# A state-space loop in which GpSimd, no longer VectorE, makes the product of delta and u, from ScalarE's copy of u

## The reference

```python
def fp_step(y_prev):
    x_tilde = (x - y_prev) @ W_mix.T + y_prev                   # "u", 256 channels
    bc = _shift1(y_prev) @ W_bc.T
    Bt = bc_normalize(B0 + bc[..., :16]); Ct = bc_normalize(C0 + bc[..., 16:])
    # h_t = exp(delta_t A) h_{t-1} + (delta_t u_t) B_t ;  y_t = sum_n h_t C_t + D u_t
    y = _selective_scan(x_tilde, delta, A, Bt, Ct, D)
    return layer_norm(y)
y_star = fori_loop(0, 8, lambda i, y: y + 0.99 * (fp_step(y) - y), zeros)
y = fp_step(y_star)
```

## Time and profile before

| | us |
|---|---|
| runs | 10309.9, 10301.13, 10301.96 |
| median | 10301.96 |
| profiled execution, time | 10288.07 |
| profiled execution, span | 10285.8 |

### The profile page before, as it was taken

How to read it: one execution, slowest core, us unless ns; L and a number is a source line. 1 busy time by engine, 2 the same in 40 slices (tenths; PEclk the granted TensorE clock), 3 DMA queues, 4 the chain that set the end, 5 groups by cost and what they waited for, 6 DMA issues and landing times.

```text
span 10285.8 us, 259086 instructions
## 1 busy us (share of the span) xinstructions
PE 9253.0 (90%) x88474; PEld 6391.3 (62%) x88474; DVE 8862.1 (86%) x16781; ACT 7235.6 (70%) x15052; POOL 6118.4 (59%) x4900
## 2 busy tenths in 40 slices
PE   7989899898998989989899899999989999899988
PEld 4656656566565665656656566565665656656566
DVE  6988979789797897978979799797997979879798
ACT  5867768677686776857768576685866858668586
POOL 1936829377293772927729277392763928639286
PEclk9999999999999999999999999999999999999999
DMA  0000000000000000000000000000000000000000
GB/s 22 0 3 1 2 3 0 3 1 2 3 0 3 1 2 3 0 3 1 2 3 0 3 1 2 3 0 3 1 2 3 0 3 1 2 3 0 3 1 3
DMA packets 648478, 23.66 MB, mean 2 GB/s; under 512 B 629185, under 2 KB 647250, under 8 KB 647506
## 3 DMA queue, kind: packets, MB, share of 16 engines
q1 hardware_dynamic: 647890, 16.11, 3.7%
HBM read 9.40 MB, written 4.19 MB: 1 GB/s over the span
## 4 chain that ended last, share of the span: by engine, by line
DVE 28%; PE 23%; issue 18%; POOL 17%; ACT 11%; DVEq 1%; POOLq 1%; DMA 0%; SPq 0%; ACTq 0%
POOL work L1714 16%; DVE work L1605 11%; DVE work L1595 6%; PE ps L605 4%; ACT scan_in L1099 4%; PE ps L595 4%; PE ps L590 3%; PE ps L534 3%; PE ps L522 2%; DVE stats L1225 1%; ACT da L985 1%; ACT yscT L1132 1%; DVE scan_in L1509 1%; POOL skip_u L1687 1%; PE ps L802 1%
## 5 line engine op out<-in xcount | busy, mean ns | idle before, releaser
L1714 POOL TENSOR_TENSOR work<-work,crep 128x512 f32<-128x512 f32 x4608 | 5765.1, 1277 | 4093.7 <-DVE work L1544 3590.7
L1099 ACT ACTIVATE scan_in<-du,bcn 128x256 f32<-128x256 f32 x8832 | 3690.6, 497 | 69.6 <-PE ps L812 36.9
L1605 DVE TENSOR_TENSOR_SCAN work<-da,hend,ps 128x256 f32<-128x256 f32 x4608 | 3028.0, 725 | 57.8 <-PE ps L812 48.7
L812 PE MATMUL ps<-w_ident,scan_in 128*128 128x128 f32 x18432 | 2455.3, 278 | 275.6 <-ACT scan_in L1099 147.0
L812 PEld LDWEIGHTS ps<-w_ident,scan_in 128*128 128x128 f32 x18432 | 2018.9, 142 | 873.6 <-DVE work L1605 324.6
L1595 DVE TENSOR_TENSOR_SCAN work<-da,ps 128x512 f32<-128x512 f32 x2048 | 2353.4, 1201 | 38.8
L802 PE MATMUL ps<-work,w_sel 128*32 128x256 f32 x17792 | 1408.7, 390 | 276.5 <-POOL work L1714 275.5
L1020 ACT ACTIVATE work<-ps,w_gate_b 128x512 f32<-128x512 f32 x512 | 349.6, 686 | 824.7 <-PE ps L590 684.4
L802 PEld LDWEIGHTS ps<-work,w_sel 128*32 128x32 f32 x17792 | 375.3, 108 | 756.7 <-POOL work L1714 541.3
L1336 DVE TENSOR_REDUCE smax<-ps 128x1 f32<-128x512 f32 x1024 | 656.9, 685 | 162.0 <-PE ps L499 158.0
L985 ACT ACTIVATE da<-ps 128x512 f32<-128x512 f32 x1024 | 555.3, 606 | 147.3 <-PE ps L522 140.4
(11 more groups left out here) (205 smaller groups left out, 12083.1 us busy)
## 6 DMA issues: line engine op xcount, KB each, us to landing
hend<-work SPq DMA_DIRECT2D x2304, 1.0 KB, 1.8
x_in<-in_x SPq DMA_DIRECT2D x17, 256.0 KB, 2.8
out<-work SPq DMA_DIRECT2D x16, 256.0 KB
gate_w<-in_gate_w SPq DMA_DIRECT2D x1, 1024.0 KB, 5.0
up_w<-in_up_w SPq DMA_DIRECT2D x1, 1024.0 KB, 7.1
down_w<-in_down_w SPq DMA_DIRECT2D x1, 1024.0 KB, 9.1
w_w_zy<-in_w_zy SPq DMA_DIRECT2D x1, 256.0 KB
work<-in_w_mix SPq DMA_DIRECT2D x1, 256.0 KB
```

The lines of the kernel that those rows point to most:

```text
L812: mm = eng.transpose(ps[:, bank, c:c + P], scan_in[:, m, tb, 2 * j + s].rearrange("p k c -> p (k c)"), ident[:])
L1099: ins = eng.activation(scan_in[:, m, tb, :, k, :], du[:, hf, tb, :].rearrange("p (e c) -> p e c", c=GC), ACT.Copy, scale=bcn[:, hf, tb, 0, ...
L1605: ins = eng.tensor_tensor_scan(hst[:, p % NHID, half], da[:, 1, 2 * p + s, :], ps[:, RING[p % 4], half], hend[:, 2 * p + s:2 * p + s + 1], ...
L1714: eng.tensor_tensor(prod[:, to, :].rearrange("p (s t) -> p s t", s=2), hst[:, p % NHID, :].rearrange("p (s t) -> p s t", s=2), crep[:, hf, ...
```

## The change

The product du moves from VectorE (behind scan 11, from PSUM) to GpSimd (behind product 10, from ScalarE's copy `u_sb`). The normalising of B and C moves from behind scan 11 to behind scan 10 on VectorE. The product D u moves from behind product 11 to behind product 13 on GpSimd. ScalarE's copy of u waits for the matmuls of u and for the D u of the unit before (which reads `u_sb`), no longer for du. TensorE's `front_c` drops its wait for du. The first unit of a sequence and the last one, outside the loop of turns, keep what they had.

```diff
-DVE_VAR, DVE_NORM, DVE_Y, DVE_BC, DVE_DU, DVE_BCN = 3, 4, 6, 8, 11, 11
-POOL_SKIP = 11
+DVE_VAR, DVE_NORM, DVE_Y, DVE_BC, DVE_BCN = 3, 4, 6, 8, 10
+POOL_DU, POOL_SKIP = 10, 13
...
                     eng.wait_ge(bc_normed.sem, bc_normed.count(at, kf + 1))
-                    eng.wait_ge(du_done.sem, du_done.count(at, kf + 1))
                     eng.wait_ge(u_copied.sem, u_copied.count(at, kf + 1))
...
             def front_keep(at, hf, kf):
-                eng.wait_ge(du_done.sem, du_done.count(at, kf + 1))
+                eng.wait_ge(u_done.sem, u_done.count(at, kf + 1))
+                eng.wait_ge(skip_done.sem, skip_done.count(at, kf))
                 eng.activation(u_sb[:], half6, ACT.Copy).then_inc(u_copied.sem, u_copied.up(at))
...
-            def front_du(at, hf, kf):
-                eng.wait_ge(u_done.sem, u_done.count(at, kf + 1))
-                eng.tensor_tensor(du[:, hf], half6, delta[:, hf * HB:(hf + 1) * HB, :],
-                                                 ALU.mult).then_inc(du_done.sem, du_done.up(at))
...
-                        if p == DVE_DU:
-                            front_du(at, other, kf)
...
         @block.gpsimd
         def _(eng):
+            def front_du(at, hf, kf):
+
+                eng.wait_ge(u_copied.sem, u_copied.count(at, kf + 1))
+                eng.tensor_tensor(du[:, hf], u_sb[:], delta[:, hf * HB:(hf + 1) * HB, :],
+                                  ALU.mult).then_inc(du_done.sem, du_done.up(at))
...
                     product(at, hf, p, p // QP, p % PROD)
+                    if p == POOL_DU and kf is not None:
+                        front_du(at, 1 - hf, kf)
                     if p == POOL_SKIP and kf is not None:
                         skip(at, 1 - hf, kf)
```

## The result

The changed kernel takes 10582.47 us (median of 4 runs, 10579.39 to 10587.74), the kernel before, run beside it, 10304.44 us. The ratio is 1.0275, 95% interval [1.026, 1.029]: 278 us slower. The forecast was 10589 us in a range of 10490 to 10650.

What follows compares the result with a forecast made beforehand. VectorE and GpSimd's chain into scan 4 were taken to bind side by side. Du's 1.25 us less leads of 0.08 and 0.18 us gave 2.24 us per turn, 287 us: 10302 + 287 = 10589 us, range 10490 to 10650.

Steps and rivals of the forecast that it cites:

- What bounds the loop: GpSimd runs without idle from product 7 to product 3; VectorE leads it at scan 4 by 0.08 and 0.18 us.
- The price of du: On GpSimd, du as one more instruction like D u takes 1.25 us, between 1.23 and 1.31.
- The gain costed at nothing: Taking du off VectorE, 1.18 us per turn, gains nothing: it becomes a wait ahead of scans 0 and 4.
- The sum: Scan 4 to scan 4: units grow 1.17 and 1.07 us, 2.24 per turn, 287 us per launch.
- The order in the stretch: On GpSimd, moving D u two products back leaves the length of the stretch without idle unchanged.
- Scan 0: Group 0's fill comes 0.5 us later, VectorE idles some 0.8 us ahead of unit one's scan 0; not added.
- A: VectorE is the bound and GpSimd takes du in its idle time: 142 us faster, 10160 us; chance 0.06.
- B: VectorE's lead is larger by du's 0.59 us, so loss and gain net: 136 us slower, 10438 us; chance 0.10.
- C: Late fill of group 0 delays ScalarE's later work, 0.8 us more per turn: 10691 us; chance 0.06.
- D: The transition into unit two absorbs more, down to nothing: 150 us slower, 10452 us; chance counted with B, 0.10.

Runs made afterwards that it cites:

- added instruction: Kernel before plus one GpSimd product of 128x512 behind product 10 of each unit, same tile as both operands, du still on VectorE: 10518 us, 1.021.
- the deferred version: Changed kernel with D u made one unit later, behind product 5 on GpSimd: 10414 us, 1.010.
- the adding runs: Kernel before plus one GpSimd product per unit: 10518 us with one tile twice, 10610 with two operands, 10592 with two operands and five idle TensorE transposes.
- remove only: Kernel before with du left out of the loop on both engines, fills reading a du made ahead of the loop: 10269 us, 0.9965.
- the best version: Changed kernel with D u one unit later, behind product 5, and du one product earlier, behind product 9: 10351 us, 1.005.
- five transposes: Kernel before plus a two-operand GpSimd product per unit and five idle TensorE transposes ahead of the old unit's last sum: 10592 us, 1.029.
- the run with everything earlier: Changed kernel, D u deferred, du behind product 9, u behind piece 10, y behind scan 5, its transposes behind piece 5, first sum behind piece 4: 10593 us, 1.028.

## Why the prediction was right

**What bounds the loop.** Right, and the best supported part: a lead of 0.26 us per turn was read; removing du gained 0.22, and the added instruction cost 2 x 1.00 - 0.25.

**The price of du.** 1.25 us estimated; by its rows 1.27 in its record and 1.23 between starts (457.29 to 458.52). Against VectorE's 665 ns it is 1.91 times as long. With 1.23 in place of 1.25 the prediction's sum gives 2.20 us per turn. The Trainium skill (SBUF — State Buffer, Who interferes with whom) says that a VectorE instruction with at most one SBUF input doesn't contend with GpSimd, outside the perf modes that use both port pairs. The trace agrees as far as it goes: unit two's scans, whose one tensor in SBUF is `da`, have a median of 1195 ns before and after. Unit one's, which read `hend` as well, have a mean of 725 ns before and 726 after. GpSimd is at work beside most scans in both kernels, so this shows only that its 2.4 us more per turn slowed none of them.

**The gain costed at nothing.** Right. VectorE has 1.18 + 2.26 = 3.44 us per turn to spare now; 2.97 of them stand in the brackets of new waits shown above, the rest in gaps too small for one. GpSimd's brackets in the turn sum to 3.1 us, where 3.3 had been forecast. They were 3.2 in the turn before, too: the 3.3 came from all 816 waits of the earlier trace rows, of which 48 lie outside the turns.

**The sum.** 2.24 us per turn forecast, 2.26 in the turn shown and 2.23 in the median; 287 us against 278, with an interval from 0.026 to 0.029 of 10304, 268 to 299 us. The mechanism is right, and a little of the closeness is luck: by its own sum the instruction's real price gives 2.20, and the first turns of a sequence grew by 0.7 us less than the sum has.

**What was read too simply.** The prediction had scan 4 held by product 1 and the first sum alone. The first sum starts 0.16 and 0.13 us behind product 1, but TensorE also comes to it straight from `back_z`, so product 15 holds it just as closely. The prediction looked for VectorE's waits ahead of scan 4 in both units. In unit one there is none (421.44, 469.80), in unit two 0.23 us; they stand mostly ahead of the moments (0.32 and 1.25). There are three ways from product 15 and product 1 to scan 4, close together: the first sum; `back_d` and `back_z` to the moments; the copy of the sums to the fill of group 1. The run with the first sum moved shows that the first isn't alone. It made no difference to the number, because all three start from GpSimd's position and shift by the same amount.

**The order in the stretch.** "Both places lie in the stretch without idle, so the order doesn't change its length" was right of the changed kernel (du alone moved: the same time) but its reason was incomplete: in the kernel before the same move costs 241 us. That stretch had no idle because D u stood where VectorE's two extras made a gap; now du stands there.

**Scan 0.** A wait of 0.8 us was forecast, 1.17 measured. From the start of piece 0 to scan 0 it was 0.94 us, where I had 0.73. It didn't count, as said; it does in the deferred version, where it is 1.88.

**The rivals.** A falls to the adding runs: 3.3 us of idle absorbed 0.25. B (netting) falls to remove only. C would have shown as some 49.1 us a turn and didn't. D falls with the distances from scan 4 to scan 4: in the changed kernel's trace they start at 421.44, 446.50 and 469.80, so 25.06 and 23.30 us; before at 414.57, 438.48 and 460.68, so 23.91 and 22.20. Both units grew, by 1.15 and 1.10 us (forecast 1.07 and 1.17). So the lead per turn is borne out, and its split into 0.08 and 0.18 isn't.

What stays open: whether a schedule exists in which du on GpSimd wins. GpSimd then needs some 45 us per turn and the best version ran at 46.50; the idle that is left lies around the layer norm, and the one attempt to move that earlier failed at ScalarE's part. Open too is why the first turn of a sequence grew less, and what besides the wait of 1.81 us decides whether the clock falls.

## What to carry to other kernels

In this kernel idle time belonged to a place, not to the engine as a whole. So before moving work to the emptier engine, find the stretch in which it runs without a bracket, and see whether the chain that ends last leaves from there. Of an engine that is 98% busy, ask how far it leads the next chain at the point where they meet; that lead (here 0.26 us of 1.18), not the work removed, is the gain. And an instruction that costs nothing may be filling a gap that another engine's work makes, so that moving it away from that gap brings out its full price.

## What the runs showed of the hardware

- A GpSimd product of 128x512 f32 took 1.04 us with the same tile as both operands and 1.31 with two different tiles (both x256, ranges 1.030 to 1.057 and 1.292 to 1.332).
- TensorE's granted clock fell in the midst of a busy loop, after a wait of 1.81 us, and cost 0.95 us in that turn. It fell in 31 of the 112 turns that have this wait. With the first added instruction the wait at this place was 1.62 us and it fell in one turn. With five transposes in it (1.12 us left), and in the changed kernel (1.31 to 1.35 us), it fell in none.
- The wait at that place isn't the only way to it: in the run with everything earlier TensorE's longest wait for anything was 1.41 us, and the clock fell in 17 of 128 turns, some 11 us into the turn.
